# Cross-attention without a key projection: two weights folded on the chip, the router's halves side by side, a new order of the step

## What is computed

```python
x = _layernorm(x + attn(x))                 # 16 heads of 16, rotary embedding
x = _layernorm(x + xattn(x, ctx_1024))      # one head of 256
x = _layernorm(x + ffn(x))                  # 16 experts, two per token, and a shared expert

def xattn(x, context, Wq, bq, Wk, bk, Wv, bv):
    q = einsum('bsd,ed->bse', x, Wq) + bq
    k = einsum('btd,ed->bte', context, Wk) + bk
    v = einsum('btd,ed->bte', context, Wv) + bv
    scores = einsum('bse,bte->bst', q, k) / sqrt(256)
    return einsum('bst,bte->bse', softmax(scores, axis=-1), v)
```

## Time and profile before

| what | value |
|---|---|
| timed runs, median of 3 | 1008.48 us |
| timed runs, lowest and highest | 1007.96 and 1017.24 us |
| span of the profiled execution (the page has no other time for it) | 1094.3 us |
| mean granted TensorE clock over the span | 0.901 |
| PE busy | 878.3 us, 80% of the span |
| DVE busy | 651.8 us, 60% |
| ACT busy | 478.9 us, 44% |
| POOL busy | 363.3 us, 33% |
| cross-attention's first instruction, and the last stage's | 403.96, 661.33 us |

### The profile page before, as it was taken

How to read it: one execution, slowest core, us unless ns; L and a number is a source line. 1 busy time by engine, 2 the same in 40 slices (tenths; PEclk the granted TensorE clock), 3 DMA queues, 4 the chain that set the end, 5 groups by cost and what they waited for, 6 DMA issues and landing times. The chain is left out here.

```text
span 1094.3 us, 19721 instructions
## 1 busy us (share of the span) xinstructions
PE 878.3 (80%) x6248; PEld 707.8 (65%) x6249; DVE 651.8 (60%) x1490; ACT 478.9 (44%) x1065; POOL 363.3 (33%) x392
## 2 busy tenths in 40 slices
PE   3588888888887876999999987730897999988994
PEld 2455555555554446888888875620687999967883
DVE  5367776767765504666666657401554777826777
ACT  1126665656655632555555532200442554522443
POOL 4322343244242003444444310777000000054772
PEclk8669999999998778999999998955899999997997
DMA  2887999899999136555555212433433555532543
GB/s 67 231 184 178 251 237 228 225 249 224 241 246 226 53 75 107 103 121 121 120 118 115 98 58 100 156 124 111 129 111 111 160 169 163 169 100 85 162 120 102
DMA packets 194421, 162.67 MB, mean 149 GB/s; under 512 B 82480, under 2 KB 179376, under 8 KB 191280
## 3 DMA queue, kind: packets, MB, share of 16 engines
q1 hardware_dynamic: 177712, 134.50, 48.5%
q0 software_dynamic: 6144, 16.79, 4.7%
q10 hardware_dynamic: 10496, 10.49, 3.2%
HBM read 81.91 MB, written 75.37 MB: 144 GB/s over the span
## 5 line engine op out<-in xcount | busy, mean ns | idle before, releaser
L601 DVE TENSOR_REDUCE neg_m<-ps_s 128x2 f32<-128x512 f32 x256 | 169.3, 688 | 44.5 <-PE ps_s L352 44.2
L488 ACT ACTIVATE probs<-ps_t 128x512 f32<-128x512 f32 x256 | 147.1, 598 | 75.8 <-PE ps_t L358 71.8
L352 PE MATMUL ps_s<-k_stack,q_stack 48*128 48x256 f32 x512 | 122.0, 343 | 54.8 <-DVE neg_m L601 41.7
L108 PE MATMUL ps_f<-w_cross,w_sgu 128*128 128x512 f32 x552 | 141.4, 403 | 22.2 <-issue 22.1
L352 PEld LDWEIGHTS ps_s<-k_stack,q_stack 48*128 48x128 f32 x512 | 78.8, 201 | 112.6 <-issue 55.2
L1950 POOL DMA_INDIRECT w_gu<-expert_outputs,pos x64 | 64.0, 1001 | 219.2 <-DMA expert_outputs<-low 200.6
L108 PEld LDWEIGHTS ps_f<-w_cross,w_sgu 128*128 128x128 f32 x552 | 105.0, 196 | 44.9 <-issue 25.1
L1524 PE MATMUL ps_f<-w_sdn,hid_hl 128*128 128x256 f32 x576 | 84.0, 297 | 50.6 <-issue 35.7
L358 PE MATMUL ps_t<-q_stack,k_stack 49*128 49x256 f32 x512 | 121.9, 342 | 2.7 <-ACT probs L488 2.7
L1524 PEld LDWEIGHTS ps_f<-w_sdn,hid_hl 128*128 128x128 f32 x576 | 79.6, 202 | 61.0 <-issue 42.1
L108 PE MATMUL ps_g<-w_qkv,x_hl 128*128 128x512 f32 (+1 forms) x384 | 91.0, 387 | 19.0 <-DVE w_qkv L527 11.1
(11 more groups left out here) (189 smaller groups left out, 1713.0 us busy)
## 6 DMA issues: line engine op xcount, KB each, us to landing
stacks<-q_hl SPq DMA_DIRECT2D x48, 256.0 KB, 2.8
stacks<-k_hl SPq DMA_DIRECT2D x48, 256.0 KB, 3.3
q_stack<-stacks SPq DMA_DIRECT2D x32, 384.0 KB, 6.4
k_stack<-stacks SPq DMA_DIRECT2D x32, 384.0 KB, 9.4
expert_rows<-no_rows ACTq DMA_DIRECT2D x16, 640.0 KB, 5.6
low<-expert_rows SPq DMA_DIRECT2D x79, 128.0 KB, 2.1
expert_outputs<-low SPq DMA_DIRECT2D x79, 128.0 KB, 1.8
heads_out<-o_sb SPq DMA_DIRECT2D x32, 256.0 KB, 9.6
```

What stands on the lines that cost most here:

```text
L108: last = pe.matmul(out, lhs(l, c), rhs(r, c), start=(n == 0), stop=(n == len(todo) - 1))
L352: by_query = pe.matmul(ps_s[n % 2][:, k * N:(k + 1) * N], q[q_rows, slab, k * P:(k + 1) * P], kk[q_rows, slab, :], start=True, stop=True)
L488: act.activation(probs[:, n % RING], ps_t[n % 2].rearrange("p (t q) -> p t q", t=TT), ACT.Exp).then_inc(exp_done, 1)
L601: dve.tensor_reduce(neg_m[c][:, :, row], ps_s[n % 2].rearrange("p (t k) -> p t k", t=TT), AX.X, ALU.max, negate=True).then_inc(max_done, 1)
```

## The change

**The key projection goes.** The scores are (x1 Wq' + bq)(c Wk' + bk)'. With A = Wq'Wk (256 by 256) they are x1 A c' plus one term per key (bq by Wk), one per query (x1 by Wq'bk) and a constant. A is made on the chip once: both weights are loaded as they are at the start of cross-attention, turned (8 transpositions), split, multiplied (12 instructions), scaled and split again into `w_fold`. XQ is now x1 by A with the per-key term as its bias (`q_bias`), and S2 multiplies it by the split context itself: `xk_f` and `xk_hl`, and XK, are gone. The per-query term needs a sum over x1 times `by_key_bias`: GpSimd multiplies (`x1u`), ScalarE sums (`row_term`), and VectorE takes it in with two operations over 128x2 behind the row maxima (`neg_m2`, `exp_bias`).

**Values.** XV is made one step later, with `b`; ScalarE copies it without the bias. The bias is added to x1 by GpSimd (`x1b`), which x2 then uses.

**Router.** High and low part of its weights stand side by side as moving operand, 2 x 18 columns, for 8 instructions instead of 12 (`router`); VectorE adds the halves in the reduction that replaces the copy of the logits.

**Heads.** The reciprocal stays on VectorE (`recips`, now for batch i + 2, at the end of the step); the product into `att` is one instruction on GpSimd.

**Self-attention** loads 11 pieces instead of 13: WkT and WqT are no longer among them.

```diff
-CROSS = ("WkT", "WvT", "WqT", "routerT")
+CROSS = ("WvT", "routerT")
@@ load, on SP
-                    sp.wait_ge(c_lo, b.n - 1)
                     sp.wait_ge(xb_done, b.n - 1)
-                sp.dma_start(cT[b.par][:], cT_dram[:, :, bass.ds(b.n * N, N)]).then_inc(cT_in[b.par], 16)
...
+                if b.least(2):
+                    sp.wait_ge(c_lo, b.n - 1)
+                sp.dma_start(cT[b.par][:], cT_dram[:, :, bass.ds(b.n * N, N)]).then_inc(cT_in[b.par], 16)
@@ TensorE
+            def fold():
+
+                pe.wait_ge(raw_in, 4 * 16)
+                for n, out in enumerate((ps[2], ps[5])):
+                    for o in range(KC):
+                        for c in range(KC):
+                            last = pe.transpose(out[:, o * D + c * P:o * D + (c + 1) * P], raw[n][:, c, part(o)], ident[:, :])
+                    last.then_inc(fold_full, 1)
+                wq, wk = nat
+                idle_products(pe, ps[1], shared.w_sgu, 6)
+                pe.wait_ge(folded, 2)
+                for q in range(KC):
+                    last = product(pe, ps[7][:, q * D:(q + 1) * D], lambda l, c: wq[:, l, c, part(q)], lambda r, c: wk[:, r, c, :])
+                last.then_inc(fold_full, 1)
...
@@ TensorE, step
+                if (i + 1).inside():
+                    pe.wait_ge(att_done, s.n + 2)
+                    turn(i, "AT", lambda o, m: att[:, m, part(o)])
+                if b.inside():
+                    pe.wait_ge(c_lo, b.n + 1)
+                    pe.wait_ge(read[bank["XQ"]], use(i, "XQ"))
+                    halves(i, "S2", N, lambda l, c, q: xq_hl[:, l, c, part(q)], lambda r, c: c_hl[b.par][:, r, c, :])
...
@@ GpSimd
+            def heads_normed(i, b):
+
+                pool.wait_ge(rec_done, b.n + 1)
+                if b.least(1):
+                    pool.wait_ge(full[bank["AT"]], use(i - 1, "AT"))
+                pool.tensor_tensor(att.rearrange("p t (d w) -> p t d w", w=HD), heads[b.par][:, :, 0:HD, :],
+                                   rec[:].unsqueeze(2).broadcast_to([P, TT, HD, HD]), ALU.mult).then_inc(att_done, 1)
...
             def step(i):
                 s, r = i, i - 2
-                if (i + 1).inside():
-                    context_lo(i + 1)
...
                 if r.inside():
                     norm_root(1, r)
+                if (i + 1).inside():
+                    heads_normed(i, i + 1)
...
                 if s.inside():
-                    pool.wait_ge(xk_hi, s.n + 1)
-                    pool.tensor_tensor(xk_hl[s.par][:, 1], xk_f[:], xk_hl[s.par][:, 0].bitcast(F32), ALU.subtract).then_inc(xk_lo, 1)
                     norm_root(0, s)
+                    if s.static and s.n == 0:
+                        pool.wait_ge(folded, FOLDS)
+                    context_lo(s)
+                    row_products(i, s)
+                    with_value_bias(i, s)
                 if (i + 1).inside():
                     residual(i, i + 1)
```

More of the change, by code:

```diff
@@ L720, in cross_attention @@
         xb = sb("xb", [TT, D])
-        rec = sb("rec", [TT, HD])
-        att = sb("att", [TT, D])
         attT = sb("attT", [KC, N])
         x1 = [sb(f"x1_{p}", [TT, D]) for p in range(2)]
+        x1b = [sb(f"x1b{p}", [TT, D]) for p in range(2)]
+        x1u = sb("x1u", [TT, D])
+        row_term = sb("row_term", [TT])
         x1_hl = sb("x1_hl", [2, KC, N], F32R)
@@ L731, in cross_attention @@
         shift = sb("shift", [TT])
-        xk_f = sb("xk_f", [KC, N])
-        xk_hl = [sb(f"xk_hl{p}", [2, KC, N], F32R) for p in range(2)]
         xq_hl = sb("xq_hl", [2, KC, N], F32R)
-        xv = [sb(f"xv{p}", [TT, D]) for p in range(2)]
+        xv = sb("xv", [TT, D])
+        neg_s = sb("neg_s", [TT])
         neg_m2 = sb("neg_m2", [TT])
+        exp_bias = sb("exp_bias", [TT])
         sum2 = sb("sum2", [TT])
@@ L869, in part, with router @@
                 return slice(q * P, (q + 1) * P)
+            def router(i):
+                out = fill(i, "LG")
+                for q in range(TT):
+                    todo = [(l, c) for c in range(KC) for l in range(2)]
+                    for n, (l, c) in enumerate(todo):
+                        last = pe.matmul(out[:, q * 2 * NR:(q + 1) * 2 * NR].rearrange("p (r e) -> p r e", r=2),
+                                         x2_hl[:, l, c, part(q)], w_rt[:, :, c, 0:NR], start=(n == 0), stop=(n == len(todo) - 1))
+                last.then_inc(full[bank["LG"]], 1)
             def gate(c):
@@ L874, in gate @@
                     pe.wait_ge(xg_first_in, 32)
-                    pe.wait_ge(read[bank["XK"]], use(Step(0, NB - 1), "XK"))
+                    pe.wait_ge(read[bank["X1T"]], use(Step(0, NB - 1), "X1T"))
                 else:
                     pe.wait_ge(shared.silu_done, c)
-                product(pe, ps[bank["XK"]][:, :], lambda l, k: shared.w_sgu[:, l, k, part(c)],
+                product(pe, ps[bank["X1T"]][:, :], lambda l, k: shared.w_sgu[:, l, k, part(c)],
                         lambda r, k: xg_first[:, r, k, :]).then_inc(shared.gate_full, 1)
@@ L913, in step @@
                 if b.inside():
-                    pe.wait_ge(xk_lo, b.n + 1)
-                    pe.wait_ge(read[bank["XQ"]], use(i, "XQ"))
-                    halves(i, "S2", N, lambda l, c, q: xq_hl[:, l, c, part(q)], lambda r, c: xk_hl[b.par][:, r, c, :])
-                if r.inside():
-                    pe.wait_ge(read[bank["X2T"]], use(i, "X2T"))
-                    halves(i, "LG", P, lambda l, c, q: x2_hl[:, l, c, part(q)], lambda r, c: w_rt[:, r, c, :])
-                    if i.static and i.n == NB:
-                        gate(0)
+                    halves(i, "XV", D, lambda l, c, q: c_hl[b.par][:, l, c, part(q)], lambda r, c: w_xv[:, r, c, :])
+                if s.inside():
+                    pe.wait_ge(x1_done, TT * s.n + TT)
+                    turn(i, "X1T", lambda o, m: x1[s.par][:, m, part(o)])
+                if i.static and i.n == NB:
+                    gate(0)
                 if b.inside():
@@ L1018, in step @@
                     act.copy(x1_hl[:, 0], chunks_of(fetch(i, "X1T"))).then_inc(x1_hi, 1)
-                if (i + 1).inside():
-                    if s.least(0):
-                        act.wait_ge(full[bank["PJ"]], use(i, "PJ"))
-                    act.copy(attT[:], chunks_of(fetch(i, "AT"))).then_inc(read[bank["AT"]], 1)
             pipe.steps(act, step)
```

284 lines of the change are left out of this document (166 added, 118 removed).

## The result

The changed kernel took 1031.40 us in the median of six runs (1018.74 to 1034.19). Six runs of the kernel before on the same chip had a median of 1015.21 (1007.96 to 1021.52): the three that the prediction started from, 1008.48, lay low. The ratio is **1.015, interval 1.010 to 1.020**: 16 us slower. Four more runs of the changed kernel beside thirteen of the one before gave 1.020 (1.009 to 1.031). The forecast was 1023, 999 to 1042.

What follows compares the result with a forecast made beforehand. TensorE's work was taken to set cross-attention's 13.51 us step. Loop wait +1.2, clock +14.3, start +5, end -3.8 and self-attention -2 gave +14.7 on 1008.5: 1023 us, range 999 to 1042.

Steps and rivals of the forecast that it cites:

- The wait for `att`: Cross-attention loop: TensorE waits at AT for GpSimd's `att`; steps 13.60 instead of 13.51 us, +1.2 us over 13 steps.
- The circle: Loop's dependency path through PV2, x2, root, `att`, AT and S2: 13.54 us, 13.6 with register instructions (13.5 to 13.8).
- The gap's size: TensorE's standstill in front of AT in each loop step: 2.96 us, more than the 2.3 us of work taken away.
- The clock: Loop: TensorE falls to half clock after the gap, 1.1 us a step, +14.3 us (0 to 21).
- My first rival: Loop: the clock stays up despite the gap, so 1023 - 14.3 = 1009 us; chance 0.24.
- The start: Start of cross-attention: weights folded before batch 0's AT, step 2 at 446.6 instead of 441.7; +5 us (2 to 9).
- The end: Cross-attention from step 15: no AT, hence no gap, and a shorter way to PV2; -3.8 us (-5 to 0).
- The rival of a dear product: Loop: GpSimd's product into `att` costs 2.6 us, not 1.3, giving 1040; chance 0.14, shared with more slow stretches.
- two slow stretches per gap: Loop: two slow-clock stretches per gap would also give 1040; chance 0.14, shared with dear GpSimd.
- AT finds `att` ready: Loop: no wait at AT, steps are TensorE's work of 10.7 us and no clock falls, giving 971; chance 0.05.
- Self-attention: Self-attention: two pieces of 256 KB no longer loaded and split; -2 us (-11 to 0).
- the late piece: Self-attention: ScalarE's 5.01 us wait for Wq's piece; rival that timed runs have it too gives 1015, chance 0.11.

Runs made afterwards that it cites:

- e1: Changed kernel with GpSimd making `att` of the next batch before the second norm's root, not behind it; 1000.48 us, ratio 0.993.
- e6: Changed kernel with AT back behind X1T on TensorE, on PJ's bank, and ScalarE's copy of it behind X1T's; 1006.54 us, ratio 0.993.
- e5: Changed kernel with GpSimd's product of heads and `rec` made twice, first into a spare tile, in front of `att`; 1072.41 us in its one run.
- e9: Changed kernel with 160 of 512 columns of GpSimd's product into `att` made additionally, into a spare tile, before it; 1035.56 us in its one run.
- e3: e1 with GpSimd making the context's low part behind the two products over x1, not in front of them; 1022.29 us, ratio 1.007.
- e10: Changed kernel with self-attention again loading and splitting the WkT and WqT pieces, which nobody uses; 1027.50 us, ratio 1.019.
- e8: e3 with SP's context load behind the stores of x2 and batch 0's start no longer behind the whole fold; 980.43 us, ratio 0.970.

## Why the prediction came out right, step by step

- **The wait for `att`** held. The circle was to be 13.6, and was 13.60 from step 4 on: 0.09 over before in each step, 1.2 us in all. e1 and e6, which each open the circle, gave 12.0 and 12.5. In e5 the gap grew by the 1.2 us put in, and the step by that and the clock's 2.2.
- **The gap's size** failed: 2.96 forecast, 2.48 measured, with the circle's length right. PJ was counted by the distance to the next product (1.54), but the profile, which models the ends of products, has TensorE busy for 1.89 before it stands still, and XQ to PJ took 1.60, not 1.41. 0.5 us too much gap. The stalls of the earlier trace rows are counted from the busy end, so the 2.96 was held against them in another unit; counted as they are it would have been 2.61.
- **The clock**, +14.3 forecast, was 2.4, and this is the step that went most wrong: steps 2 and 3 took 14.75 and 14.87 (S2 2.71 and 2.68); the others lost none. e9 shows that the same step with a gap of 2.95 would have paid the 1.1 a step. The gap's length isn't all of it: steps 2 and 3 had the same gap as the rest (2.53 and 2.46). A start with stretches at half clock lies just before them; whether that is the reason isn't shown. The stalls of the earlier trace rows, shorter than 2.48, didn't carry over as a bound; the prediction's own rival puts that down to other short waits around them, which no run tested. The rule of the Trainium skill ("TensorE: Matmul & The Clock Gate", section "HAM oscillation — how this bites in real kernels"), which warns only of idle gaps longer than all of these, agrees with the changed kernel from step 4 on; it doesn't with steps 2 and 3, nor with e9, where gaps of 2.95 us were enough. My first rival ("the clock stays up") was the truer mechanism.
- **The start** was too cheap: +5 forecast, +9.0 measured. The loads landed 8.9 and 8.8 us after the begin (forecast 9.5). The fold up to AT took 13.1 and 11.1 (11.5), from there to step 1 10.4 and 10.9 (9), and step 1 took 15.8 and 13.2 us where 12.6 was forecast: XQ, PJ and PV2 ran at half clock in the first profile, XQ alone in the second. One term was missed: x1's normalisation took 1.67 there, beside GpSimd's context part.
- **The end**, -3.8 forecast: -2.1. Step 15 took 11.95 instead of 10.7, of which 0.99 is a wait for x1; step 16 up to PV2 11.6 instead of 12.4.
- **Router**: 8 products of 36 columns from start to PV2 0.97 us (forecast 0.9). **GpSimd's product** 1.27 (1.30). The rival of a dear product falls, and with it the two slow stretches per gap, for 1040. *AT finds `att` ready* falls with the first bullet.
- **Self-attention**, -2 forecast; -3.1 in the profiles, which can't be put down to the pieces: cross-attention began anywhere from 390.9 (e9) to 404.5 us (e3) in kernels with the same self-attention, and at 399.98 in e10, which has the pieces back. The prediction's argument against a cost of the late piece, that the timed runs are 86 us shorter, fell too: ScalarE's wait (4.79) was there in an execution of 1014.1 us.
- **The last stage**, for which nothing was forecast, was 1.9 shorter.
- **The base** was 3 to 7 us low: 1008.48 for what four later groups of 7 to 25 runs put at 1011.2 to 1015.4.

So 1023 was near 1031 in part by luck, because errors balanced: the clock 12 us too much, start and end 6 too little, the base 3 to 7 too low; and 5 to 8 us of the timed difference no profile shows. What rests on what was right is that the change didn't make the kernel faster: TensorE's 2.3 us of saved work were turned wholly into a wait. That it came out slower by over 1% doesn't rest on it. The prediction had that from its clock term; with the 2.4 us that the clock cost, its own sum gives 1008.5 + 2.8 = 1011, within 1%. The runs have it from the start (+9.0), the loop (+3.8) and the part that no profile shows.

## What to carry to other kernels

Work taken from the bound engine only counts if no product that it issues early waits for something made late in the same step: walk the circle through every engine's order before moving an instruction ahead. Here the change's gain was there all along, and three reorderings (heads before the root, context last, stores before the load) brought 1025 to 985 us (1.020 to 0.972 of the kernel before); each uncovered the next wait, and the middle one alone lost 15 to 22. When a gap's length decides something, take it from the engine's busy end, not from the distance between starts, and hold it only against gaps counted the same way.

## What the runs showed of the hardware

- GpSimd held VectorE up: two instructions over 128x256 in SBUF took 1.77 us beside a GpSimd subtraction in SBUF, and 0.73 alone; the subtraction kept its 1.29. The Trainium skill, "SBUF — State Buffer", section "Who interferes with whom", says that one pair of ports is shared by the two and held for a whole instruction; these rows agree, and e3, which parts the two instructions, had 0.74 again. I hadn't priced this. Not every pair is hit: the statistics of x2, SBUF only as well, kept their 0.75 us beside `att`.
- The same wait at nearby lengths, in the same place of the same step, left the mean granted clock from 480 to 600 us at 1.00 (2.48 us) or took it to 0.90 (2.95 us) and 0.82 (3.69 us), and with it 0, 1.1 and 2.2 us a step. The last two are one execution each. The length alone doesn't decide: in steps 2 and 3 gaps of 2.53 and 2.46 us were followed by half clock (S2 2.71 and 2.68 us), and in e9 one of 2.96 us (at 537.60) by full clock.
- Products with one moving column and 32-bit operands took 0.106 us each from start to start (16 in 1.70, at 413.49 in the changed kernel), little less than 36 columns in the router (8 in 0.97, 0.12 each). In e8, where the products around them were slow too, the 16 took 3.27 us (from 418.58).
